# Running sums on two halves of the edges, with every fourth sum stored, in a two-layer graph kernel

## The reference

```python
aggregated = segment_sum(edge_attr, dst, num_segments=3125)      # [3125, 64]
h = swish(concat([x, aggregated, u[0]]) @ W1 + b1)
x = layernorm(x + swish(h @ W2 + b2))
```

## Time and profile before

| | us |
|---|---|
| median of 3 runs | 2944.01 (2944.01 to 2948.17) |
| the profiled execution, its time | 2940.88 |
| its span, first to last instruction | 2938.7 |
| PE / DVE / ACT / POOL busy | 2457.7 / 2590.5 / 1518.8 / 1911.2 |

### The profile page before, as it was taken

The page is one execution under the profiler, slowest core; times in us unless marked ns, Lnnn a source line. Parts: engine busy times, 40 slices in busy tenths (PEclk is TensorE's granted clock), DMA queues, the critical chain, the costliest instruction groups (busy, mean ns, idle before and its releaser), DMA issues. The chain is left out here.

```text
span 2938.7 us, 48472 instructions
## 1 busy us (share of the span) xinstructions
PE 2457.7 (84%) x12897; PEld 1776.8 (60%) x12897; DVE 2590.5 (88%) x3389; ACT 1518.8 (52%) x2914; POOL 1911.2 (65%) x1719
## 2 busy tenths in 40 slices
PE   2233358999999999999999999999999999999714
PEld 1232325667766666777677776777777777777511
DVE  6688735899999999999899999999999999999737
ACT  1321224565656655666565665666666666666410
POOL 2700037777777777777777777777777777777130
PEclk8555558999999999999999999999999999999855
DMA  6787713244444445444444444544444544544440
GB/s 187 211 221 189 208 27 103 75 128 145 145 143 143 140 140 149 145 142 146 141 142 145 143 145 140 148 144 146 145 147 142 147 144 145 145 146 141 120 139 11
DMA packets 229767, 415.36 MB, mean 141 GB/s; under 512 B 61999, under 2 KB 89059, under 8 KB 225830
## 3 DMA queue, kind: packets, MB, share of 16 engines
q1 hardware_dynamic: 169638, 296.66, 32.6%
q0 software_dynamic: 52704, 107.19, 14.9%
q10 hardware_dynamic: 7128, 8.13, 0.8%
HBM read 309.59 MB, written 102.20 MB: 140 GB/s over the span
## 5 line engine op out<-in xcount | busy, mean ns | idle before, releaser
L749 POOL DMA_INDIRECT gathered<-xtab_d,src_g x784 | 886.9, 1131 | 297.6 <-issue 216.6
L749 POOL DMA_INDIRECT gathered<-qtab_d,dst_g x784 | 877.6, 1119 | 254.5 <-issue 245.2
L1127 PE MATMUL bank<-z_h,wt_h 128*128 128x512 f32 x1568 | 729.1, 465 | 38.0 <-DVE val L1586 34.3
L879 ACT ACTIVATE z_h<-xa_t 128x512 fp32r<-128x512 f32 x980 | 616.7, 633 | 104.5 <-DVE xa_t L1553 77.1
L1553 DVE TENSOR_TENSOR xa_t<-bank,r_r 128x512 f32<-128x512 f32 x980 | 667.2, 682 | 1.7 <-PE bank L1155 1.7
L1129 PE MATMUL bank<-z_h,wt_l 128*128 128x512 f32 x1568 | 619.7, 395 | 0.0
L1128 PE MATMUL bank<-z_l,wt_h 128*128 128x512 f32 x1568 | 618.9, 395 | 0.0
L1561 DVE TENSOR_TENSOR z_l<-xa_t,z_h 128x1024 fp32r<-128x1024 f32 x392 | 476.6, 1216 | 43.9 <-ACT z_h L879 43.8
L1127 PEld LDWEIGHTS bank<-z_h,wt_h 128*128 128x128 f32 x1568 | 300.1, 191 | 145.6 <-issue 109.9
L1155 PE MATMUL bank<-s,sel 128*128 128x512 bf16 x980 | 349.2, 389 | 8.8 <-issue 4.3
L873 ACT ACTIVATE hid<-bank,b1kv 128x512 f32<-128x512 f32 x196 | 135.1, 689 | 407.2 <-PE bank L1111 407.2
(11 more groups left out here) (222 smaller groups left out, 4210.9 us busy)
## 6 DMA issues: line engine op xcount, KB each, us to landing
nrow_d<-x_r SPq DMA_DIRECT2D x196, 288.0 KB
ea<-in_ea_t SPq DMA_DIRECT2D x392, 128.0 KB
exb<-exd_d SPq DMA_DIRECT2D x196, 256.0 KB
dmb<-exd_d SPq DMA_DIRECT2D x196, 256.0 KB
ea_c<-in_ea_t SPq DMA_DIRECT2D x49, 512.0 KB, 5.0
aggrow_d<-xa_t SPq DMA_DIRECT2D x49, 512.0 KB, 3.9
gathered<-xtab_d,src_g POOLq DMA_INDIRECT x784
gathered<-qtab_d,dst_g POOLq DMA_INDIRECT x784
```

What stands on the lines that cost most here:

```text
L749: rows_in = pool.indirect_dma_start(rows[:, c % 4, k, :], None, table, bass.IndirectOffsetOnAxis(ap=picked[:, s, at:at + 1], axis=0))
L879: act.activation(z_h[:, c % 2, i, :], z[:, i, :], ACT.Copy).then_inc(zh_ok, 1)
L1127: pe.matmul(ps[:, :], wt_h[rows, w, :], high, start=start, stop=False)
```

## The change

The edges are cut into two halves of EH = 50176, on partitions 0 to 63 and 64 to 127, and a chunk is W = 1792 edges of each half: NC is now 28. The scan adds the edge first and multiplies by the flag of the edge after it (`keep_d` is read one place further), so a sum is zero at a node's last edge. Of the sums only every fourth is transposed (four transposes of 112 columns a chunk), copied (once) and stored in `sums_d`. For each node three things are then added: the stored sum just before the last group of four edges (`lead_i`, gathered by POOL after the last chunk, masked by `led`), the last four edges themselves (`quads`, gathered by POOL from `ea_rows` while the scans run, masked by `mine` and added up), and, for the node that lies across the two halves, the first half's last sum (`mid_b`). The flags are stored first, the harmonics and `x` are loaded after two chunks of edges, runs 0 and 1 stand between the `is_le` passes, the seven small loads of `dst_d` (`piece_last`, `line_i`) move from SP to ScalarE's queue ahead of `split`. In the loop, ScalarE and VectorE do the same operations in another order. The branch for unsorted inputs is adapted; it is not taken.

```diff
-W = 2048
-NC = EP // W
+EH = EP // 2
+W = 1792
+NC = EH // W
+CQ = 4
+WJ = 4
+WP = W // (CQ * WJ)
+KEEP_AT = 63
...
+            def load_edges(c, b):
+                lo = c * W
+                for half in range(2):
+                    sp.dma_start(ea_c[half * D:(half + 1) * D, b, :], edges_t[:, bass.ds(lo + half * EH, W)]
+                                 ).then_inc(chunk_in[b], 16)
+            def load_keeps(c, b):
+                lo = c * W
+                for half in range(2):
+                    sp.dma_start(keep_c[half * D:(half + 1) * D, b, :],
+                                 keep_d[bass.ds(lo + half * EH + KEEP_AT + 1, W)].rearrange("(o w) -> o w", o=1)
+                                 .to_broadcast([D, W])).then_inc(chunk_in[b], 16)
+            def load_chunk(c, b):
+                sp.wait_ge(chunk_run, c - (CR - 1))
+                load_edges(c, b)
+                load_keeps(c, b)
+            def store_chunk(c, b):
+                sp.wait_ge(chunk_row, c + 1)
+                sp.dma_start(sums_d.rearrange("(r h) d -> r (h d)", h=2)[bass.ds(c * (W // CQ), W // CQ), :]
+                             .rearrange("(p j) d -> p (j d)", p=WP), row_c[:, b, :]).then_inc(chunk_out[b], 16)
+            load_edges(0, 0)
+            sp.wait_ge(flags_done, 1)
+            sp.dma_start(keep_d[KEEP_AT:KEEP_AT + EP].rearrange("(p c) -> p c", p=P), keep[:, :]
+                         ).then_inc(flags_out, 16)
...
+            sp.wait_ge(flags_out, 32)
+            load_keeps(0, 0)
+            load_edges(1, 1)
+            load_keeps(1, 1)
+            sp.dma_start(shf, harmonics_t.rearrange("s (c w) -> (s c) w", c=SC)).then_inc(sh_in, 16)
+            sp.dma_start(x_r[:, :, 0:D], a["x"].rearrange("(t p) d -> p t d", p=P)).then_inc(x_in, 16)
...
+            sp.dma_start(mid_b[:, :], sums_d[EH // 2 - 2:EH // 2 - 1, :].to_broadcast([P, D])).then_inc(mid_in, 16)
...
+                pool.wait_ge(quad_ok, 2)
+                pool.wait_ge(split_done, 3)
+                for t in range(NT):
+                    pool.indirect_dma_start(quad_rows[:, t, :, :].rearrange("p i w -> p (i w)"), None,
+                                            edge_rows.rearrange("(r i) w -> r (i w)", i=CQ),
+                                            bass.IndirectOffsetOnAxis(ap=quad_i[:, t:t + 1], axis=0)
+                                            ).then_inc(quads_in, 16)
...
+                dve.tensor_tensor_scan(run_c[:, b, :], ea_c[:, b, :], keep_c[:, b, :], run_c[:, 1 - b, W - 1:W],
+                                       ALU.add, ALU.mult).then_inc(chunk_run, 1)
...
             for k in range(RP):
+                if k == 3:
+                    run(0)
+                if k == 5:
+                    run(1)
...
+            run(NC - 6)
+            run(NC - 5)
+            dve.wait_ge(quads_in, 16 * NT)
+            run(NC - 4)
+            dve.tensor_tensor(flat, flat, across(mine[:, :, :].rearrange("p t i -> p (t i)"), D, 1), ALU.mult
+                              ).then_inc(quad_step, 1)
...
+            run(NC - 3)
+            dve.wait_ge(quad_step, 10)
+            for i in range(2):
+                dve.tensor_tensor(edges_of[:, :, i, :], edges_of[:, :, i, :], edges_of[:, :, 2 + i, :], ALU.add
+                                  ).then_inc(quad_step, 1)
+            run(NC - 2)
...
+                dve.tensor_tensor(x_r[:, tiles, D:2 * D], x_r[:, tiles, D:2 * D], edges_of[:, tiles, 0, :], ALU.add
                                   ).then_inc(masked, 1)
```

The loop, on ScalarE and then on VectorE:

```diff
             def body(j, c):
+                if live(j, c - 1):
+                    scores_high(j, c - 1)
                 if live(j, c + 1):
                     front_h(j, c + 1)
...
                     outer_high(j, c + 1, 1)
+                if live(j, c + 1):
+                    weights_v(j, c + 1)
+                    outer_high(j, c + 1, 2)
                 s = batch_at(c, 10)
                 if live_batch(j, s):
                     batch_turned(j, s)
-                if live(j, c - 1):
-                    scores_high(j, c - 1)
                 if live(j, c + 1):
-                    weights_v(j, c + 1)
-                    outer_high(j, c + 1, 2)
                     outer_high(j, c + 1, 3)
...
                     weigh(j, c - 1)
+                if live(j, c):
+                    outer_low(j, c, 2)
...
                     outer(j, c + 1, 2)
+                    outer(j, c + 1, 3)
                     key_query(j, c + 1)
-                    outer(j, c + 1, 3)
...
                     edge_low(j, c + 2)
-                if live(j, c + 1):
-                    outer_low(j, c + 1, 2)
```

More of the change, by code:

```diff
@@ L315, in gnn_two_layers @@
         ends_ok = sem("ends_ok")
+        quad_step = sem("quad_step")
+        quad_ok = sem("quad_ok")
+        quads_in = sem("quads_in")
+        mid_in = sem("mid_in")
+        led_ok = sem("led_ok")
+        own_ok = sem("own_ok")
         chunk_in = [sem(f"chunk_in{i}") for i in range(CR)]
@@ L801, in _, with split @@
             act.activation(head_sel[:, BP - H:BP], headones[:, bass.ds(0, H, DH)], ACT.Copy).then_inc(head_ok, 1)
-            act.wait_ge(sh_in, 16)
-            for part in range(3):
+            def split(part):
                 if part > 0:
@@ L1033, in _ @@
             pe.matmul(bank[5][0:D, 448:449], w1u[:, :], u0[:, :], start=True, stop=True).then_inc(b1e_ps, 1)
-            pe.wait_ge(cuts, 1)
-            pe.matmul(bank[6][:, 0:PIECES], ones[0:1, :], l_line, start=True, stop=True).then_inc(cuts_ps, 1)
             pe.wait_ge(find_step, 4)
@@ L1419, in _ @@
                               ).then_inc(cuts, 1)
[L1421 to L1450 removed]
+            run(2)
+            run(3)
             sh_remainder(1)
[L1452 removed]
+            with dve.Fori(1, CL // 2) as i:
                 for r in range(CR):
@@ L1463, in _ @@
             dve.tensor_reduce(within[:, :], rows[0], AX_X, ALU.add).then_inc(find_step, 1)
-            dve.tensor_reduce(has[:, :], rows[1], AX_X, ALU.max).then_inc(ends_ok, 1)
+            dve.tensor_reduce(own_f[:, :], rows[1], AX_X, ALU.add).then_inc(own_ok, 1)
+            dve.wait_ge(own_ok, 1)
+            dve.tensor_scalar(has[:, :], own_f[:, :], 1.0, None, ALU.min).then_inc(ends_ok, 1)
             dve.wait_ge(find_step, 9)
@@ L1488, in _ @@
+            dve.wait_ge(own_ok, 5)
+            dve.tensor_tensor(mine[:, :, :], across(iota_row[:, 0:CQ], NT, 2), across(own_f[:, :], CQ, 1), ALU.is_gt
+                              ).then_inc(own_ok, 1)
+            dve.wait_ge(own_ok, 6)
+            dve.tensor_tensor(mine[:, :, :], mine[:, :, :], not_past[:, :, :], ALU.mult).then_inc(own_ok, 1)
+            dve.wait_ge(own_ok, 7)
+            with dve.Fori(CL // 2, CL - 3) as i:
                 for r in range(CR):
                     run(2 + r, i)
-            for c in range(2 + CL * CR, NC):
-                run(c)
+            edges_of = quad_rows
```

311 lines of the change are left out of this document (178 added, 133 removed).

## The result

2816.99 us (median of 3 runs, 2815.99 to 2819.88) against 2944.01; ratio 0.9566, 95% interval 0.9544 to 0.9588, so 4.3% faster. The forecast was 2802, its range 2750 to 2860. The profiled execution took 2816.0 us for a span of 2814.2; it is set beside the one before, 2940.9 for 2938.7, a difference of 124.5 us in the span.

The account below looks back on a forecast made before the run. Sums paced by DMA transfers, not VectorE; in the loop three engines within 3% of the period. 2940.9 - 109 (before the loop) - 33 (loop) = 2799, median 3.1 above: 2802 us, range 2750 to 2860.

Parts of the forecast that it names:

- Chunk 2 has landed: Head of the sums: chunk 2's load, issued near 53 us, was to be in before run(2), with no wait.
- B: Rival, sums: chunks run at 5.2 us because two halves together load faster; 14 us sooner, 2788; chance 0.11.
- E: Rival, sums: the two halves load one after the other, period 7.3 us; 19 us later, 2821; chance 0.07.
- the pace of all bytes: Sums: a chunk's 1.38 MB at 264 GB/s with DMA engines 85.4% busy gives a period of 6.1 us.
- The cross-check: Sums: a load must land in 8.3 us, 2.3 later than now; its further 0.51 MB take 1.9 at 264 GB/s.
- the walk: Step-by-step timeline of the sums from the first scan at 26 us to the last scan's end at 252.3.
- The quads: Sums after the index block: 25 gathers, 3.3 MB, were to add 9 us, plus 2 waiting for the last.
- One 0.43 us step, hidden but once: Node layer: each block adds one 0.43 us step, hidden in all but one block; 0.5 us in all.
- both waits: Loop: VectorE's two waits of 0.6 us, for `scores_high` and the key weights, go; 0.17 us a group, 33 us.
- Rival C: Loop: a group reaches 11.35 us, VectorE's busy sum; 72 us gained, 2763; chance 0.10.
- Rival A: Loop stays: POOL's pace holds every group at 11.7 us; 2835; chance 0.20.
- Rival D: Loop: ScalarE's new head, `scores_high`, waits for `weigh` and delays its chain; 150 us slower, 3094; chance 0.02.

Follow-up runs that it names:

- half_the_edges: Changed kernel without the upper half's edges from chunk 2 on (16 of 1792 columns loaded), so it leaves out work; 2795.6 us, one run.
- no_quads: Changed kernel without the 25 gathers of quads and the wait for them, two partitions filled from an input instead; 2803.9 us, one run.
- loop_old: Changed kernel with the order of before in the loop on both ScalarE and VectorE; 2841.2 us, ratio 0.9636.
- loop_new: Kernel before the change with only the new order of ScalarE and VectorE in the loop; 2913.7 us, ratio 0.9882.

## Why the prediction was right, point by point

**The head.** run(0) at 26, run(1) at 37, run(3) ending at 70.5: measured 25.6, 36.3, 73.2. "Chunk 2 has landed" was 1.4 us off. That the flags' early store would free VectorE was right.

**The period.** 6.1 us forecast, 6.18 measured beside row gathers: B (5.2) and E (7.3) are both out. I had put the landing of a load at 8.3, 2.3 longer than before; it is 8.4. But the main reason given, the pace of all bytes with the engines 85.4% busy, was not the right one: with 16% of the bytes gone the period fell by 5% at most, and the engines were 95% busy. That this sum met 6.1 was luck. The cross-check beside it was nearer to what happens: 6.0 us plus the time of the load's further bytes. What E took for proportional has a part that doesn't grow, 2.9 us or more, and that decides against it. This bears on the Trainium skill (SBUF — State Buffer, "Can I just issue two DMAs to hit both halves?"), too: the page's 196 GB/s for 64 partitions gives 5.9 us for the loads alone, by estimate. Without gathers the trace has 1.147 MB of loads in a period of 5.73, 200 GB/s, which is close. But that is with the stores, for which the prediction came to 6.7, and half_the_edges has 0.69 MB in 5.08, 135 GB/s, so the period is not the loads' bytes at one pace. Whether the two halves wait for each other, as that page says, no run here shows.

**The stage to run(24).** Runs 6 to 13 were to end at 136 and ended at 145.4, the largest miss on the way. VectorE waited 7.6 us ahead of the scan at 96.2 and 4.3 ahead of the next; the walk let the full pace begin at once. The load of the first of them went out beside the third store of the harmonics (issued at 86.9) and POOL's row gathers; that these slowed it was not tried. The index block took 17.4 (162.8 - 145.4) where I had 18.4. The quads, 9 us and 2 of waiting in my sum, cost 6.8 against the changed kernel's own trace (no_quads), with no wait. From the end of the index block to run(24) it took 64.1 us, where I had 69.6. The two misses have opposite signs, and that they nearly cancel is luck. So run(24) starts at 226.9, not 224, the last scan ends at 254.4, not 252.3, and the leads' first gather is at 259.5, not 257.5: 2 us.

**The node layer.** From that gather to the first `weigh` I had 116.2, measured 121.5, and this is most of the stage's miss. "One 0.43 us step, hidden but once" failed: in the timelines of the two kernels laid side by side the node layer is 0.7 late at the first mask, where the middle row comes later, and 4.4 late behind the last one. The add of each of the seven blocks stands on VectorE between the mask and TensorE's turning of the block, in a chain that runs from block to block: the last masks are 7.25 us apart in place of 6.8. In the other runs with this node layer the stretch takes 120.8 to 124.9 us, so the last 1 us is not assigned.

Together: 101.9 gained where 109 were forecast.

**The loop.** 33 us forecast, 21.4 measured; with the other kernels that have this loop, 19 to 28. The mechanism was right, both waits went: 37.2 and 16.1 us of VectorE's idle time became 1.8 and 0. The size was off because I let them go without anything in their place, 0.17 us a group. Ahead of `weigh`, the moved `outer_low(2)` and the five `outer` VectorE now idles 58.4 us (30.5 + 12.6 + 15.3), 18.6 in loop_old (18.1, 0 and 0.5); ahead of the other two `outer_low` (`z_l`) it idles 14.5 less. The steady seven went from 81.27 to 80.36 us, 0.13 a group where I had 0.17. Rival C is closed: TensorE is now busy for 80.3 of 81.0. Rival A falls with loop_old and loop_new, since the order alone makes 81.26 into 80.36; POOL's 0.32 pauses stayed as they were, and it did not hold the steady part. Earlier in the loop TensorE waits 11.1 us for its gathers. Rival D's chain did not form: ScalarE's new head alone was not slower than loop_old (0.9626 against 0.9636).

2799 + 7.1 (stage) + 11.6 (loop) - 1.2 (behind the loop) = 2816.5, and the profiled execution took 2816.0.

## What to carry to other kernels

Where two buffers pace a loop, measure issue to landing and split it into a fixed and a growing part before scaling it: storing a sixteenth of the sums or a second queue did next to nothing here, a smaller load did. A step that was added to each block of a chain cost its length in every block here, however idle its engine is on average. When two waits of an engine that is 97% busy were removed here, about half of their length was gained (51.5 us of waits, 25.5 of the loop against loop_old): the next wait stood close behind. And compare single traces only beyond the spread of kernels that are the same in that stretch, or by a part that repeats: by whole-loop means ScalarE's order looked like half of the gain, in the steady seven it was a tenth.

## What the runs showed of the hardware

One DMA over 128 partitions, with its source in two halves by a pattern of three dimensions, was three times slower than two DMAs of 64: 19.0 us a chunk in place of 6.2, with 18.8% of the engines' time in use and two of its packets in flight at a time. The engines' busy share is no measure of room either: at 90% for the queue from 104 to 142 us, moving 8.19 MB, an engine's busy time was spent at 15 GB/s (0.899 x 16 x 38 us), and in the slow form at 24 (0.188 x 16 x 114 us): packets last longer when all the engines work, those of 7168 bytes 490 ns on average from 104.4 to 141.5 in place of 279. And writing a loop out, without its branch, did not make it faster.
